# A one-layer language-model tower: the score operands of batch 0 transposed on TensorE instead of restacked by DMA, with unused products between TensorE's work

## The chip, the cores and the metric

One core of a Trainium2 chip runs the program. The metric is the device time of one execution in microseconds (us).

## The reference

For 8 batches of 256 token ids the program looks up rows of 256 in an embedding table, adds a 16-head attention (head width 16, rotary positions) of the normalised rows, and adds a mixture of 8 experts of which the best one by a gate is used.

```python
h = _L0_tok_ref(x, embeddings)                       # rows of the table: (8, 256, 256)
h = h + _L0_attn_ref(_layernorm(h), w_qkv, w_proj)   # q, k rotated; softmax(q k / 4) v; w_proj
h = h + _L0_ffn_ref(_layernorm(h), gate_w, expert_w) # x + expert_w[argmax(gate)] x, x normalised
```

## The kernel before

**The work of one batch.** Each batch has two tiles of 128 tokens (t = 0, 1). GpSimd gathers the rows (`gather`, L321 to L329). VectorE takes the statistics (`f_norm_a`) and, after GpSimd's reciprocal root (`f_rs_of`), scales (`f_norm_b`). TensorE transposes the rows (`x_transpose`, L426). Products are made exact enough by parts: ScalarE rounds to fp32r (`x_high`), VectorE takes the rest (`x_low`), and `product` (L417) adds high by high, low by high and high by low, for two halves of the contraction: six matmuls of 512 columns for `project_qk` of a tile, twelve of 256 columns for `project_v` of a batch.

**Rotation and restack.** `rotate(b, t)` is two VectorE products with the cosine and sine tables out of PSUM (L846, L850), and `rotated_sum` on GpSimd (L342) adds them into `qk`. `qk_transpose` turns it on TensorE (four transposes), `qk_high` and `qk_high_again` on ScalarE and `qk_low` on VectorE fill `parts`, and `restack(b)` (L271), six DMAs of 256 KB from the SP queue, spreads `parts` into `stacks[b % 3]`, where each head of 16 has its high and low parts and a repeat on 48 partitions. In this form one matmul over 48 partitions gives the whole score of a head. Two more rows hold the maxima (`maximum` on SP, or ScalarE's queue for the first) and ones (`ones_rows`).

**Steps, slots and visits.** The steady work is a loop of steps of 16 slots, from step -1. In step b, eight visits (`visit`, L522, one every second slot) each do two heads: the transposed scores of batch b, whose exponentials ScalarE takes (L731), and the plain scores of batch b + 1 into two PSUM banks, whose row maxima VectorE takes (`maximum`, L863). Each bank is written again only when its maximum is out. `max_split`, `max_transpose` and `max_row` turn the negated maxima into rows. Every fourth slot sixteen products of 32 columns make the outputs (`outputs`, L543). Tables (`FRONT`, `EARLY`, `ONE`, `TWO`, L169 to L173) say in which slot each piece of a later batch is issued; each engine runs its own list in order, and waits are on semaphores. Experts of batch b - 2 run in step b, from step 2 on.

**The opening.** Ahead of the loop each engine has a list written out by hand: TensorE L672 to L688, ScalarE L792 ff., VectorE L1002 ff., GpSimd L395 to L408, SP L248 ff. Batches 0, 1 and 2 are projected there. The restack of batch 0 is awaited by the first scores, in step -1:

```python
def scores_wait(b, v, half):
    if v == 0:
        wait(pe, stack_in, b * 96 + 96)
    wait(pe, max_ok, b * NH + 2 * v - half)
```

Step -1 is the scores and maxima of batch 0 alone, step 0 the first with exponentials. `qk_high(1, t)`, which writes `parts` again, waits for the restack of batch 0 (L708).

## Time and profile before

| | us |
|---|---|
| median of three runs | 322.32 |
| lowest and highest | 320.94 and 324.34 |
| the profiled execution | 324.0 |
| its span, first to last instruction | 322.2 |
| TensorE busy in it | 280.8 (87%) |
| VectorE busy | 243.8 (76%) |
| ScalarE busy | 127.0 (39%) |
| GpSimd busy | 85.7 (27%) |

Mean granted clock of TensorE in the profiled execution: 0.944. PE is TensorE's matmuls, PEld its weight loads, DVE VectorE, ACT ScalarE, POOL GpSimd, SP the engine that issues most DMAs; a q behind an engine's name is its instruction queue. L and a number is a line of the kernel. Times count from the first instruction. Busy times are of the engine, and an idle engine costs only where others wait for it.

### The profile page before, as it was taken

To read this page: it belongs to the slowest core of one execution; us is meant where nothing else is said; L and a number is where in the kernel's file an instruction comes from. 1 tells how busy PE (TensorE), PEld (TensorE's weight loads), DVE (VectorE), ACT (ScalarE), POOL (GpSimd) and SP (SyncE) were. 2 spreads that over 40 slices of the span, in tenths; PEclk is the share of its full clock that TensorE was granted. 3 is DMA by queue.
4 is the path that set the end of the run, shared out by engine and by line. 5 is a ranking of instruction groups with operands and counts; after the bars stand their busy time and mean duration, and the time that the engine had idled before them with its cause. 6 is when DMAs were issued, how large, how long until landed. Compare 5 with 4: busy or idle time off the path is not lost.

```text
span 322.2 us, 5465 instructions
## 1 busy us (share of the span) xinstructions
PE 280.8 (87%) x2000; PEld 201.1 (62%) x2000; DVE 243.8 (76%) x595; ACT 127.0 (39%) x261; POOL 85.7 (27%) x96
## 2 busy tenths in 40 slices
PE   0388489888878999989998999999999999999894
PEld 0267367454655777667765776676766766667582
DVE  6766667667798879887997799687988974657663
ACT  3032213643766543345343444353535435330100
POOL 4743500013567402250234113400210210210301
PEclk9999775558999999999999999999999999999998
DMA  4269492480191084015600470039000000001000
GB/s 115 73 247 149 66 161 28 83 119 1 25 161 27 9 142 58 4 36 113 91 6 32 92 117 4 0 94 139 4 33 4 1 28 10 3 1 35 0 33 33
DMA packets 11590, 19.14 MB, mean 59 GB/s; under 512 B 2012, under 2 KB 4903, under 8 KB 11436
## 3 DMA queue, kind: packets, MB, share of 16 engines
q1 hardware_dynamic: 10776, 18.23, 30.4%
q0 software_dynamic: 768, 0.55, 0.7%
q8 instruction: 16, 0.26, 0.3%
q14 instruction: 10, 0.08, 0.1%
q10 hardware_dynamic: 20, 0.02, 0.0%
HBM read 5.30 MB, written 2.10 MB: 23 GB/s over the span
## 4 chain that ended last, share of the span: by engine, by line
PE 47%; DVE 26%; issue 11%; POOL 5%; DMA 4%; ACT 4%; SPq 1%; POOLq 0%; DVEq 0%; ACTq 0%
PE e_bank L422 13%; PE o_bank L552 7%; DVE neg_max L863 7%; PE f_bank L422 7%; DVE acc L942 5%; PE t_pair L517 5%; DMA stacks<-parts 3%; PE s_pair L488 3%; POOL qk L342 2%; PE s_pair L422 2%; PE m_bank L564 2%; PE m_bank L422 2%; POOL res L360 2%; PE o_bank L422 1%; ACT parts L695 1%
## 5 line engine op out<-in xcount | busy, mean ns | idle before, releaser
L731 ACT ACTIVATE probs<-t_pair 128x512 f32<-128x512 f32 x128 | 69.7, 596 | 91.4 <-PE t_pair L517 91.0
L863 DVE TENSOR_REDUCE neg_max<-s_pair 128x2 f32<-128x512 f32 x128 | 82.0, 684 | 15.0 <-PE s_pair L488 15.0
L488 PE MATMUL s_pair<-stacks 48*128 48x256 f32 x256 | 54.8, 341 | 5.8 <-DVE neg_max L863 2.8
L517 PE MATMUL t_pair<-stacks 50*128 50x256 f32 x256 | 50.0, 325 | 2.0 <-DVE neg_max L863 1.7
L517 PEld LDWEIGHTS t_pair<-stacks 50*128 50x128 f32 x256 | 35.5, 199 | 24.4 <-issue 21.4
L422 PE MATMUL e_bank<-ew_h,y_h 128*128 128x512 f32 x92 | 40.3, 439 | 4.6 <-DVE acc L938 2.7
L488 PEld LDWEIGHTS s_pair<-stacks 48*128 48x128 f32 x256 | 38.9, 209 | 8.8 <-DVE neg_max L863 5.0
L552 PE MATMUL o_bank<-probs,vals 128*32 128x256 f32 x512 | 36.4, 405 | 1.2 <-ACT max_rows L695 1.2
L942 DVE SCALAR_TENSOR_TENSOR acc<-e_bank,mask,acc 128x256 f32<-128x256 f32 x66 | 28.9, 479 | 11.2 <-PE e_bank L422 11.2
L422 PE MATMUL e_bank<-ew_h,y_l 128*128 128x512 f32 x92 | 36.3, 395 | 0.0
L422 PE MATMUL e_bank<-ew_l,y_h 128*128 128x512 f32 x92 | 36.3, 395 | 0.0
L342 POOL TENSOR_TENSOR qk<-rope_a,rope_b 128x512 f32<-128x512 f32 x16 | 20.7, 1292 | 49.8 <-DVE rope_b L850 49.7
L422 PEld LDWEIGHTS e_bank<-ew_h,y_h 128*128 128x128 f32 x92 | 17.3, 188 | 12.0 <-DVE acc L942 3.9
L552 PEld LDWEIGHTS o_bank<-probs,vals 128*32 128x32 f32 x512 | 14.0, 113 | 14.9 <-issue 7.5
L422 PE MATMUL f_bank<-wqkv_h,x_h 128*128 128x512 f32 (+1 forms) x44 | 17.2, 390 | 4.7 <-DVE x_l L834 3.8
L349 POOL TENSOR_SCALAR g_ve<-g_mv 128x2 f32<-128x2 f32 x8 | 2.0, 248 | 67.9 <-DVE g_mv L820 67.9
L422 PEld LDWEIGHTS e_bank<-ew_l,y_h 128*128 128x128 f32 x92 | 17.3, 188 | 4.2
L695 ACT ACTIVATE o_t<-o_bank 128x256 f32<-128x256 f32 x32 | 12.4, 389 | 16.1 <-PE o_bank L552 16.1
L335 POOL TENSOR_SCALAR f_ve<-f_mv 128x2 f32<-128x2 f32 x8 | 2.4, 296 | 61.6 <-DVE f_mv L820 61.6
L422 PEld LDWEIGHTS e_bank<-ew_h,y_l 128*128 128x128 f32 x92 | 17.4, 189 | 2.1
L325 POOL DMA_INDIRECT h<-in_emb,ids x16 | 17.2, 1076 | 5.5 <-issue 3.4
L360 POOL TENSOR_TENSOR res<-acc 128x512 f32<-128x512 f32 x8 | 10.2, 1276 | 31.0 <-DVE acc L942 31.0
(132 smaller groups left out, 532.1 us busy)
## 6 DMA issues: line engine op xcount, KB each, us to landing
stacks<-parts SPq DMA_DIRECT2D x48, 256.0 KB, 7.0
ew_raw<-in_expert_w SPq DMA_DIRECT2D x1, 2048.0 KB, 8.2
out<-res SPq DMA_DIRECT2D x8, 256.0 KB, 2.1
probs<-in_w_qkv SPq DMA_DIRECT2D x2, 384.0 KB, 3.8
stacks<-max_rows SPq DMA_DIRECT2D x30, 8.0 KB
h<-in_emb,ids POOLq DMA_INDIRECT x16, 2.6
probs<-in_w_proj SPq DMA_DIRECT2D x1, 256.0 KB, 2.6
stacks<-ones SPq DMA_DIRECT2D x6, 16.0 KB
```

The source lines that it names most:

```text
L325: g.indirect_dma_start(h0[:, j, :], None, emb, bass.IndirectOffsetOnAxis(ap=ids[:, j:j + 1], axis=0), bounds_check=V - 1, oob_is_err=False ...
L342: g.tensor_tensor(qk[:, t, :, :, :].rearrange("p g d j -> p g j d"), rope_a[:, t, :, :].rearrange("p (g j) d -> p g j d", j=8), rope_b[:, ...
L360: g.tensor_tensor(res[:, :, :], acc[:, 0, :, :], acc[:, 1, :, :], ALU.add).then_inc(res_ok, 1)
L422: m = mm(o, a(c), w(c), start=(n == 0), stop=(n == 3 * C - 1))
L488: m = mm(s_pair[:, half, t * N:(t + 1) * N], stacks[b % STACKS][r:r + KS, pair, 0, t * P:(t + 1) * P], stacks[b % STACKS][r:r + KS, pair, ...
L517: m = mm(t_pair[:, half, c * N:(c + 1) * N], stacks[b % STACKS][r:r + KM, pair, 1, c * P:(c + 1) * P], stacks[b % STACKS][r:r + KM, pair, ...
L552: m = mm(o_bank[STRIP * j:STRIP * (j + 1), 0:N], vals[b % VALS][:, c, head(4 * g + j), :], probs[:, (4 * g + j) % RING, c, :], start=(c == ...
L564: m = tr(strips_bank(b, t)[:, g * P:(g + 1) * P], o_t[:, g, t * P:(t + 1) * P], ident[:, :])
L695: return nc.scalar.activation(o, i, ACT.Copy)
L731: nc.scalar.activation(probs[:, (2 * v + half) % RING, :, :].rearrange("p c n -> p (c n)"), t_pair[:, half, :], ACT.Exp, scale=SCALE).then ...
L863: v.tensor_reduce(neg_max[:, k // 4, :, 4 * half + k % 4], s_pair[:, half, :].rearrange("p (t n) -> p t n", t=NT), AX.X, ALU.max, negate=T ...
L942: v.scalar_tensor_tensor(out=acc[:, j, t, :], in0=y, scalar=mask[:, p, t, e:e + 1], in1=base[:, t, :] if u == 0 else acc[:, j, t, :], op0= ...
```

## The change

1. The score operands of batch 0 no longer go through `qk_transpose`, `parts` and `restack(0)`. ScalarE (`z_high`, three copies of 256 elements a tile), VectorE (`z_low`, two subtractions a tile) and GpSimd (`again_k`, one copy a tile) write high, low and repeated parts side by side into `zs` (the memory of `stacks[2]`), with ones beside them. `z_transpose(t)` on TensorE turns 16 blocks a tile into four banks, and eight `z_copy` on ScalarE put them into `stacks[0]`.
2. The restack of batch 1 goes in two halves of four head pairs, six DMAs of 128 KB each, with a semaphore for each; visits 0 and 4 of its scores wait for one each.
3. `fill(o, n)`: n products of 512 columns whose result nobody reads, in TensorE's list: 13 and 4 in the opening, 2 at four further places of it, and 2 behind each visit of step 0.
4. The hand-written lists are reordered: step -1 is now written out between the projections of batches 1 and 2. The rotation, transposes and values of batch 2 move from the opening into slots 0 to 5 of step 0, `proj_weights_low` moves from VectorE to GpSimd, and batch 1's normalised rows use `y_h[0]`, `y_l[0]`.

```diff
+        TWO = dict(rotate0=0, rotate1=1, t0=2, low0=3, t1=3, low1=4, v=5)
...
-            return SLOTS * (k - 2) + table[what] if k and what in table else None
+            table = {2: TWO, 3: EARLY}.get(k, FRONT)
+            return SLOTS * (k - 2) + table[what] if k > 1 and what in table else None
...
+
+        Z_BANKS = [[m_bank, o_bank, f_bank, e_bank], [s_bank[0], s_bank[1], t_bank[1], m_bank]]
+        Z_ORDER = [(0, 0), (0, 1), (1, 0), (1, 1), (1, 2), (0, 2), (0, 3), (1, 3)]
+
+        def z_copied(t, q):
+
+            return Z_ORDER.index((t, q)) + 1
+
+        def z_part(t, k, s):
+
+            return zs[:, :, k, t * P:(t + 1) * P].rearrange("p j (i r) -> p i j r", i=2)[:, :, :, s * HD:(s + 1) * HD]
+
+        def z_from(t, k):
+
+            return qk[:, t, 2 * k:2 * k + 2, :, :].rearrange("p i d j -> p i j d")
...
+            def first_restack():
+
+                sp.wait_ge(qkh_ok, NT)
+                for u in range(2):
+                    for i in range(3):
+                        if i == 1 and u == 0:
+                            sp.wait_ge(again_ok, NT)
+                            sp.wait_ge(qkl_ok, NT)
+                        for half in range(2):
+                            r = 64 * half
+                            sp.dma_start(
+                                stacks[1][r + i:r + KS:3, 4 * u:4 * u + 4, :, :].bitcast(F32).rearrange("d j k n -> d j (k n)"),
+                                parts[64 * u:64 * u + 64, half, 2 * i:2 * i + 2, :].bitcast(F32)).then_inc(half_in[u], 16)
+
...
-                ones_rows(i)
-            restack(0)
+            ones_rows(1)
+            sp.wait_ge(zt_ps, 8)
+            ones_rows(2)
+            first_restack()
...
+                    pool.wait_ge(z_hi, 2 * t + 2)
+                    pool.wait_ge(z_dup_q, t + 1)
+                    pool.wait_ge(z_dup_k, t + 1)
+                    pool.wait_ge(z_lo, 2 * t + 2)
+
...
+            def proj_weights_low():
+                pool.wait_ge(wp_h_ok, 1)
+                g.tensor_tensor(wp_l[:, :, :], wp_raw, wp_h[:, :, :].bitcast(F32), ALU.subtract).then_inc(wp_l_ok, 1)
+
+            def again_k(t):
+                wait(pool, rotated, t + 1)
+                g.tensor_copy(z_part(t, 1, 1), z_from(t, 1)).then_inc(z_dup_k, 1)
 
             def step(b, p):
                 for s in range(SLOTS):
@@ -398,14 +449,15 @@
             gather_tile(3)
             gather(2)
             f_rs_of(1)
+            gate_weights()
+            proj_weights_low()
             rotated_sum(0, 0)
+            again_k(0)
             rotated_sum(0, 1)
+            again_k(1)
             f_rs_of(2)
             rotated_sum(1, 0)
             rotated_sum(1, 1)
-            gate_weights()
-            rotated_sum(2, 0)
-            rotated_sum(2, 1)
             steps(step)
...
+            def fill(o, n):
+
+                for i in range(n):
+                    mm(o[:, :], wqkv_h[:, 0, 0:P], wqkv_h[:, 0, 0:512], start=True, stop=True)
 
+            def z_transpose(t):
+                wait(pe, z_unit, 1)
+                wait(pe, z_lo, 2 * t + 2)
+                wait(pe, z_dup_q, t + 1)
+                wait(pe, z_dup_k, t + 1)
+                if t == 0:
+                    wait(pe, xl_ok, 2)
+                    wait(pe, roped, 2 * NT)
+                for q in range(4):
+                    if t == 1 and q == 2:
+                        wait(pe, roped, 2 * NT + 2)
+                    if t == 1 and q == 3:
+                        wait(pe, z_in, z_copied(0, 0))
+                    for n in range(4):
+                        m = tr(Z_BANKS[t][q][:, n * P:(n + 1) * P].bitcast(F32R),
...
             def scores_wait(b, v, half):
-                if v == 0:
-                    wait(pe, stack_in, b * 96 + 96)
+                if b == 0 and v == 0:
+                    wait(pe, z_in, z_copied(1, 1))
+                elif b == 0 and v in (4, 6):
+                    wait(pe, z_in, max(z_copied(0, v // 2), z_copied(1, v // 2)))
+                elif b == 1 and v % 4 == 0:
+                    wait(pe, half_in[v // 4], 96)
+                elif v == 0:
...
-                    if b == -1 and s == 2:
-                        project_v(2)
+                        if b == 0:
+                            fill(m_bank, 2)
...
             pe.wait_ge(ident_ok, 1)
+            pe.wait_ge(wqkv_h_ok, 1)
+            fill(s_bank[0], 13)
             x_transpose(0)
+            fill(s_bank[0], 4)
             project_qk(0, 0)
+            x_transpose(1)
             project_qk(0, 1)
+            project_qk(1, 0)
+            pe.wait_ge(identr_ok, 1)
+            z_transpose(0)
+            z_transpose(1)
+            visit(-1, 0)
+            project_qk(1, 1)
+            visit(-1, 1)
             project_v(0)
-            x_transpose(1)
-            qk_transpose(0, 0)
-            qk_transpose(0, 1)
-            project_qk(1, 0)
-            project_qk(1, 1)
+            visit(-1, 2)
+            qk_transpose(1, 0)
+            qk_transpose(1, 1)
+            pe.wait_ge(roped, 2 * 2 * NT)
+            fill(t_bank[0], 2)
+            visit(-1, 3)
             project_v(1)
             x_transpose(2)
-            qk_transpose(1, 0)
+            max_transpose(0, 0)
+            visit(-1, 4)
             project_qk(2, 0)
-            qk_transpose(1, 1)
+            visit(-1, 5)
             project_qk(2, 1)
-            pe.wait_ge(identr_ok, 1)
+            visit(-1, 6)
+            fill(t_bank[0], 2)
+            visit(-1, 7)
+            pe.wait_ge(xl_ok, 3)
+            fill(m_bank, 2)
             steps(step)
...
+            def z_high(t):
+                wait(act, rotated, t + 1)
+                for k in range(2):
+                    copy(z_part(t, k, 0), z_from(t, k)).then_inc(z_hi, 1)
+                copy(z_part(t, 0, 2), z_from(t, 0)).then_inc(z_dup_q, 1)
+
+            def z_copy(t, q):
+                wait(act, zt_ps, 4 * t + q + 1)
+                copy(stacks[0][:, 2 * q:2 * q + 2, :, t * P:(t + 1) * P].rearrange("p j k n -> p (j k) n"),
+                     Z_BANKS[t][q][:, :].rearrange("p (m n) -> p m n", m=4)).then_inc(z_in, 1)
...
             x_high(0)
-            values(0)
-            qk_high(0, 0)
-            x_high(1)
-            qk_high(0, 1)
-            qk_high_again(0, 0)
-            qk_high_again(0, 1)
-            values(1)
-            x_high(2)
+            act.wait_ge(gw_in, 16)
+            copy(gw_parts[:, :, 0, :], gw_raw[:, :, :]).then_inc(gw_h_ok, 1)
             act.wait_ge(wp_in, 16)
             copy(wp_h[:, :, :], wp_raw).then_inc(wp_h_ok, 1)
-            act.wait_ge(gw_in, 16)
-            copy(gw_parts[:, :, 0, :], gw_raw[:, :, :]).then_inc(gw_h_ok, 1)
+            x_high(1)
+            z_high(0)
+            z_high(1)
+            for t, q in Z_ORDER:
+                z_copy(t, q)
+            values(0)
+            qk_high(1, 0)
+            qk_high(1, 1)
+            qk_high_again(1, 0)
+            qk_high_again(1, 1)
+            values(1)
+            max_row(0, 0)
+            x_high(2)
             steps(step)
...
+            def z_low(t):
+                for k in range(2):
+                    wait(dve, z_hi, 2 * t + k + 1)
+                    v.tensor_tensor(z_part(t, k, 1 + k), z_from(t, k), z_part(t, k, 0).bitcast(F32),
+                                    ALU.subtract).then_inc(z_lo, 1)
...
+            v.memset(unit[:, :], 1.0).then_inc(filled, 1)
+            dve.wait_ge(filled, 1)
+            v.tensor_copy(zs[:, :, :, :].rearrange("p j k (t i r) -> p (j k t i) r", t=NT, i=2)[:, :, KS:],
+                          unit[:, :].rearrange("p (o r) -> p o r", o=1).broadcast_to([P, 64, HD])).then_inc(z_unit, 1)
+            qkv_weights_low()
             f_norm_a(0)
-            qkv_weights_low()
             f_norm_b(0)
             dve.wait_ge(ident_ok, 1)
             v.tensor_copy(ident_r[:, :], ident[:, :]).then_inc(identr_ok, 1)
+            f_norm_a(1)
+            x_low(0)
+            f_norm_b(1)
             for i in range(VALS):
                 v.memset(vals[i][:, :, :, HD:STRIP], 0.0).then_inc(h_zero, 1)
-            x_low(0)
-            f_norm_a(1)
-            f_norm_b(1)
             rotate(0, 0)
+            x_low(1)
+            f_norm_a(2)
             rotate(0, 1)
-            f_norm_a(2)
-            qk_low(0, 0)
-            x_low(1)
-            qk_low(0, 1)
+            z_low(0)
+            z_low(1)
+            rotate(1, 0)
             f_norm_b(2)
-            rotate(1, 0)
+            maximum(0, 0)
             rotate(1, 1)
+            maximum(0, 1)
+            qk_low(1, 0)
+            maximum(0, 2)
+            qk_low(1, 1)
+            maximum(0, 3)
+            max_split(0, 0)
             x_low(2)
             dve.wait_ge(h_zero, NB + VALS)
             for i in range(VALS):
                 v.memset(vals[i][:, :, :, HD:HD + 1], 1.0).then_inc(filled, 1)
-            proj_weights_low()
-            rotate(2, 0)
-            rotate(2, 1)
+            for k in range(4, VISITS):
+                maximum(0, k)
             steps(step)
```

## Rows read from the trace of the kernel before

**Rows 1.** The page, busy tenths in 40 slices of 8.05 us: TensorE, and its granted clock.
```profile
PE   0388489888878999989998999999999999999894
...
PEclk9999775558999999999999999999999999999998
```

**Rows 2.** Windows of 2 us: length, busy (instructions) by engine, PEclk, DMA share, GB/s.
```profile
34.00:36.00 2.00, 0.00 (x0) 0.00 (x0) 1.29 (x2) 0.00 (x0) 1.45 (x2) 1.00 0.41 65
...
46.00:48.00 2.00, 1.66 (x9) 0.99 (x8) 1.84 (x5) 0.37 (x1) 0.00 (x0) 0.80 1.10 144
...
74.00:76.00 2.00, 2.00 (x25) 1.20 (x18) 1.38 (x3) 0.46 (x1) 0.96 (x1) 0.87 0.00 0
...
78.00:80.00 2.00, 0.60 (x6) 0.36 (x4) 1.97 (x5) 1.44 (x3) 1.26 (x1) 1.00 0.01 4
```

**Rows 3.** The chain that ended last, opening: start us, us, what.
```profile
26.98 9.67 DMA stacks<-parts
```

**Rows 4.** Timeline of the opening: start us, us, engine, line, what [idle before <-releaser].
```profile
11.56 1.57 DVE L1010 MEMSET vals<- 128x512 f32 x3
...
14.11 0.76 PE L422 MATMUL f_bank<-wqkv_h,x_h 128*128 128x512 f32 x1 [1.50 <-DVE x_l L834]
...
16.80 0.63 PE L422 MATMUL e_bank<-wqkv_h,x_h 128*128 128x512 f32 x1
...
21.18 0.75 DVE L817 BATCH_NORM_STATS2 f_st<-h 128x6 f32<-128x256 f32 x2 [0.30 <-DMA h<-in_emb,ids]
...
23.71 18.93 SPq L280 DMA_DIRECT2D stacks<-parts  x12
...
24.09 0.50 PE L422 MATMUL f_bank<-wqkv_h,x_h 128*128 128x512 f32 x1 [1.05 <-DVE x_l L834]
...
25.59 0.40 PE L422 MATMUL e_bank<-wqkv_h,x_h 128*128 128x512 f32 x1
...
25.79 0.69 DVE L846 TENSOR_TENSOR rope_a<-f_bank,rope_sb 128x512 f32<-128x512 f32 x1 [0.52 <-PE f_bank L422]
...
26.40 0.68 DVE L850 TENSOR_TENSOR rope_b<-f_bank,rope_sb 128x512 f32<-128x512 f32 x1
...
28.43 0.60 PE L436 MATMUL m_bank<-ident,xn 128*128 128x128 f32 x4
...
36.79 0.68 PE L488 MATMUL s_pair<-stacks 48*128 48x256 f32 x4 [2.79 <-DMA stacks<-parts]
```

**Rows 5.** Timeline of the end of the opening and step 0.
```profile
47.58 1.91 ACTq L723 DMA_DIRECT2D stacks<-max_rows  x2
...
52.19 0.55 PE L517 MATMUL t_pair<-stacks 50*128 50x256 f32 x1 [0.28 <-DVE neg_max L863]
...
53.52 1.11 PE L477 MATMUL f_bank<-ident,qk 128*128 128x128 f32 x4
...
59.21 1.93 PE L552 MATMUL o_bank<-probs,vals 128*32 128x256 f32 x16
```

**Rows 6.** Timeline, the end of step 0 and the start of step 1.
```profile
77.27 0.38 PE L517 MATMUL t_pair<-stacks 50*128 50x256 f32 x1
...
78.74 1.28 POOL L342 TENSOR_TENSOR qk<-rope_a,rope_b 128x512 f32<-128x512 f32 x1 [2.40 <-DVE rope_b L850]
...
78.78 1.27 DVE L872 TENSOR_TENSOR max_parts<-neg_max,max_parts 128x16 fp32r<-128x16 f32 x1
...
80.73 1.07 PE L552 MATMUL o_bank<-probs,vals 128*32 128x256 f32 x16
```

**Rows 7.** The page's groups: busy us, mean ns | idle before, releaser.
```profile
L863 DVE TENSOR_REDUCE neg_max<-s_pair 128x2 f32<-128x512 f32 x128 | 82.0, 684 | 15.0 <-PE s_pair L488 15.0
...
L342 POOL TENSOR_TENSOR qk<-rope_a,rope_b 128x512 f32<-128x512 f32 x16 | 20.7, 1292 | 49.8 <-DVE rope_b L850 49.7
...
L695 ACT ACTIVATE o_t<-o_bank 128x256 f32<-128x256 f32 x32 | 12.4, 389 | 16.1 <-PE o_bank L552 16.1
```

**Rows 8.** Instructions that touch the stacks: duration ns min/median/max, first and last start.
```profile
L723 ACTq DMA_DIRECT2D stacks<-max_rows x2: 626/938/1251, 47.6 to 48.9; - x2
```

More of the change, by code:

```diff
@@ L147, in tower @@
             sem, "roped rotated qkt_ps qkh_ok qkl_ok again_ok ones_ok".split())
+        z_unit, z_hi, z_dup_q, z_dup_k, z_lo, zt_ps, z_in = map(
+            sem, "z_unit z_hi z_dup_q z_dup_k z_lo zt_ps z_in".split())
         ones_in = sem("ones_in")
+        half_in = [sem("half_in0"), sem("half_in1")]
         stack_in = sem("stack_in")
@@ L196, in steps, with turned_bank, x_parts @@
         def steps(step):
-            for b in range(-1, NB + 2):
+            for b in range(NB + 2):
                 step(b, b % 2)
+        def turned_bank(k, t):
+            return e_bank if early(k) and t == 1 else f_bank
         def front_bank(k, t):
-            return e_bank if early(k) and t == 1 else f_bank
+            return t_bank[t] if k == 1 else turned_bank(k, t)
         def x_bank(k):
             return m_bank if k in (1, 2) else f_bank
-        def turned_bank(k, t):
-            return t_bank[t] if k == 1 else front_bank(k, t)
         def v_bank(k):
-            return o_bank if k < 3 else f_bank
+            return o_bank if k < 2 else f_bank
+        def x_parts(k):
+            return (y_h[0], y_l[0]) if k == 1 else (x_h, x_l)
+        Z_BANKS = [[m_bank, o_bank, f_bank, e_bank], [s_bank[0], s_bank[1], t_bank[1], m_bank]]
[6 more added lines that the diff above has]
+            return qk[:, t, 2 * k:2 * k + 2, :, :].rearrange("p i d j -> p i j d")
         def maxima_slot(b):
@@ L275, in restack @@
                     if i == 1:
[L276 to L277 removed]
+                        wait(sp, again_ok, (b - 1) * NT + NT)
+                        wait(sp, qkl_ok, (b - 1) * NT + NT)
                     for half in range(2):
@@ L302, in ones_rows @@
                     sp.dma_start(stacks[i][r:r + 2, :, 1, :].bitcast(F32), ones[:, :]).then_inc(ones_in, 16)
-            for i in range(STACKS):
-                ones_rows(i)
-            restack(0)
+            ones_rows(1)
+            sp.wait_ge(zt_ps, 8)
+            ones_rows(2)
+            first_restack()
             steps(step)
@@ L439, in project_v @@
             def project_v(b):
-                if b >= 3:
-                    wait(pe, qkl_ok, b * NT + NT)
-                else:
-                    wait(pe, v_ok, b)
+                if b >= 2:
+                    wait(pe, qkl_ok, (b - 1) * NT + NT)
+                elif b == 1:
+                    wait(pe, v_ok, b)
+                else:
+                    pe.wait_ge(z_in, z_copied(0, 1))
+                x_h, x_l = x_parts(b)
                 for t in range(NT):
@@ L472, in qk_transpose @@
                 else:
-                    wait(pe, qkh_ok, b * NT + 1)
-                    wait(pe, qkl_ok, b * NT + 1)
+                    wait(pe, qkh_ok, (b - 1) * NT + 1)
+                    wait(pe, qkl_ok, (b - 1) * NT + 1)
                 wait(pe, rotated, b * NT + t + 1)
@@ L698, in x_high @@
                 wait(act, xt_ps, b + 1)
-                wait(act, v_ps, b)
-                copy(x_h[:, :, :, :].rearrange("p c t n -> p (c t n)"), x_bank(b)[:, :]).then_inc(xh_ok, 1)
+                wait(act, v_ps, 1 if b == 2 else 0 if b == 1 else b)
+                copy(x_parts(b)[0][:, :, :, :].rearrange("p c t n -> p (c t n)"), x_bank(b)[:, :]).then_inc(xh_ok, 1)
             def values(b):
@@ L706, in qk_high @@
             def qk_high(b, t):
-                wait(act, qkt_ps, b * NT + t + 1)
-                wait(act, stack_in, b * 96)
+                wait(act, qkt_ps, (b - 1) * NT + t + 1)
+                if b == 2:
+                    for u in range(2):
+                        wait(act, half_in[u], 96)
+                wait(act, stack_in, (b - 2) * 96)
                 copy(parts[:, :, HIGHS, t * P:(t + 1) * P].rearrange("p i k n -> p k i n"),
@@ L841, in rotate @@
                 wait(dve, qk_ps, b * NT + t + 1)
-                if b == 2:
-                    wait(dve, rotated, 1 * NT + t + 1)
+                if b in (1, 2):
+                    wait(dve, rotated, (b - 1) * NT + t + 1)
                 src = front_bank(b, t)[:, :].rearrange("p (h d) -> p h d", d=HD)
@@ L853, in qk_low @@
             def qk_low(b, t):
-                wait(dve, qkh_ok, b * NT + t + 1)
+                wait(dve, qkh_ok, (b - 1) * NT + t + 1)
                 v.tensor_tensor(parts[:, :, LOWS, t * P:(t + 1) * P].rearrange("p i k n -> p k i n"),
```

63 lines of the change are left out of this document (32 added, 31 removed).

## The prediction

> **What bounds the kernel now.** I read the page's forty slices first, then the chain, the timeline of the opening, and two-microsecond windows.
>
> The slices [rows 1] show TensorE nearly full from about 80 us on, and two weak stretches before it: the opening, in which TensorE is empty or half used, and slices five to nine, in which its granted clock reads 0.7 and 0.5. Behind them nothing is touched by the change, so it can win only ahead of step 1, which begins at 77.27 [rows 6].
>
> The chain [rows 3] says what ends last in the opening: the restack of batch 0, six DMAs of 256 KB, lands 9.67 us after its last issue. The first scores start on it at 36.79 [rows 4]. Step 0 (the first exponentials) starts at 52.19 [rows 5], so the scores of batch 0 alone take 15.4 us and step 0 takes 25.1 us.
>
> The windows [rows 2] show the clock. From 34 to 36 TensorE ran nothing and behind that the clock fell. From 46 to 48, with only score products and two small transposes, it fell again (0.80) although TensorE was busy 1.66 of 2 us. It came back in 74 to 76, behind the projection of batch 3. From 78 to 80 TensorE was busy 0.60 us with transposes, and the clock stayed at 1.00. Of the two levels, 1.2 and 2.4 GHz, step 0 ran nearly whole at the lower one. Ahead of 20 us the record reads 1.00, but six products of 512 columns then took 2.69 us from start to start of the next six (14.11 to 16.80), against 1.50 later (24.09 to 25.59) [rows 4]: that was the lower level too.
>
> **The opening up to the first score.** The restack of batch 0 goes; in its place come rounding on ScalarE and VectorE, 32 transposes, and eight copies. The first fills run where TensorE is empty, so they cost nothing and lift the clock for project_qk(0): that saves 1.2 us for each six products. It isn't on the new path, because VectorE now clears three value tiles (1.57 us [rows 4]) ahead of rotate(0, 0). The new path begins at the gather of batch 2, which landed at about 21.1 (VectorE waited for it) [rows 4], I take it because the load of the expert weights ran beside it, and still does. VectorE's order puts its statistics (0.75, and some 0.2 for the rest) ahead of rotate(0, 1): 22.1. The two rope products take 1.3 [rows 4]: 23.4. GpSimd's sum takes 1.29 [rows 7].
>
> Here z_low(0) on VectorE meets that sum, and both read two SBUF operands. The trace has the case [rows 6]: a VectorE subtraction of 16 elements took 1.27 us because it began 0.04 us behind a GpSimd sum of 1.28. So one of them holds the other; I take z_low's first half (0.4, as the 256-element activation [rows 7]) ahead of the sum and its second half behind it: the sum ends at 25.1, z_low(0) at 25.5. By the Trainium skill (SBUF — State Buffer, Who interferes with whom) such an operation contends with a GpSimd one that reads SBUF and the second is fully blocked; without the rule the sum would be 0.4 us shorter. By it, the trace agrees.
>
> z_high(1) is three activations of 256 elements, 3 x 0.39: 26.3. z_transpose(0) can start at 25.5, with TensorE empty since project_qk(1, 0) ended at about 21.7. No transpose of fp32r between these tiles is in the trace. The nearest rows are four fp32 transposes in 0.60 at the upper level and in 1.11 at the lower one [rows 4, 5]. Bounds for 32: 3 us (nothing but the columns at the rate of the 512-column products) and 8.9 us (32 x 0.28). I take 0.12 each, about a quarter of the 0.60 less the time of the last one's draining, so 3.8 us: 29.3. Six copies overlap them and the fourth is out at 29.1. First scores: 29.4, which is 7.4 us earlier than 36.79.
>
> **From the first score to step 0.** VectorE paces this. Its work from 26.5 is about 16 us: 16 maxima of 0.64 (0.68 alone [rows 7]), two rotations of batch 1 (2.6), two subtractions of 0.7, x_low(2) 0.65, the norm 0.75 and small ones. What it waits for adds 8.6 us. Step by step: the first maximum from 30.0 to 31.2; rotate(1, 1), behind project_qk(1, 1) of 1.5, to 32.9; the next maximum to 34.1; then qk_low(1, 0) stands in line and waits for visit(-1, 2), the transposes (0.6) and ScalarE's copy (0.6), to 35.8. Two subtractions and two maxima: 39.6; the split: 40.0. Now x_low(2) stands in line ahead of the other four maxima. It waits for project_v(1), x_transpose(2) and max_transpose(0, 0) on TensorE (40.7), then on ScalarE for max_row and its two DMA issues (1.91 [rows 5]) ahead of x_high(2): 43.8. x_low ends at 44.4, and project_qk(2, 0) was waiting for it as well. The last four maxima, with two projections between them, take 6.5 us. Step 0 starts at about 50.6: 21.2 us behind the first score instead of 15.4, so 5.8 us of the 7.4 are given back. The restack of batch 1, issued at 36.4 to 44.5, is hidden: the whole restack of batch 0 took 12.9 us from its first issue at 23.71 to its landing at 36.65 [rows 3, 4], so this one is down by 49.4 even from 36.4, and its first half by about 43.5.
>
> **Step 0.** Before, this ran at the lower level. At the upper one three groups of 16 output products save 0.86 each (1.93 and 1.07 [rows 5, 6]), three groups of four transposes 0.5 each, project_qk(3, 0) 1.2, and seven visits, taken to scale like the outputs (1.2 to 0.7), 3.5: in all 8.8 us. Against it stand 16 fills of 512 columns at 0.235 (3.8 us), project_v(2), moved here (12 products of 256 columns, half of the 512-column rate, 1.45), and rotate(2, 0) and (2, 1), also moved here. These hold VectorE 2.6 us and make TensorE wait at visit 1 and, for GpSimd's 1.29, at qk_transpose(2, 1): 2.2 us. 8.8 - 3.8 - 1.45 - 2.2 = 1.3 us saved, 23.8 us. The restack of batch 2 is issued in three steps, the last at about 60.4. The one before needed 12.9 us from the first issue, so it is down by 71, ahead of the end of step 0 at 74.4. gather(3) now runs in step 0, 5 us ahead of its use. proj_weights_low on GpSimd is hidden: GpSimd has nothing between 16 and 19.5.
>
> **Sum.** -7.4 + 5.8 - 1.3 = -2.9 us. The profiled execution took 324.0 (span 322.2), so it would be 321.1; that execution lies 1.7 above the median of 322.32. Beside the median the forecast is 319.4 us.
>
> **Rivals.** 1. The two long waits are shorter than worked out: the gather lands by 20 and ScalarE's DMA issues don't hold x_high(2). For: of the 1.91 the first issue took 1.25 and the second 0.63 [rows 8], so half may be a start-up; against: ScalarE's queue is in order. 1.0 + 1.9 + about 1.1 of the small gaps: -4 us, 315.4.
> 2. Slower: the clock is lost between project_qk(1, 0) and z_transpose(0). TensorE is empty there for some 3.8 us with no fill. For: 34 to 36 [rows 2] was such a gap, and the clock fell. Against: what stands around it here is denser. Then the 32 transposes cost 0.25 each (+4.1), project_qk(1, 1) and project_v(0) 1.2 more each, and visits 0.5: +7.0, 326.4. It decides from 2.9 us on, which the transposes alone exceed.
> The Trainium skill (TensorE: Matmul & The Clock Gate, Part 4: PE-mode transpose) says that transposes don't count as a busy TensorE in the same way. That speaks for this rival. The trace differs in part: from 78 to 80 [rows 2] little but transposes ran and 1.00 was kept. By the rule the time would be 326.4, by the row 319.4.
> 3. The fills don't hold the clock in step 0, so they cost double (7.2 us) and the 8.8 us aren't saved: with the second rival 335 or more.
> 4. The restack in halves moves at half the rate, since each DMA reads 64 partitions. Then its second half lands at about 59, qk_high(2, 0) waits for it, 3 us: 322.4. The kernel before has no such DMA; from 49 to 59 are the bounds.
>
> **How the numbers follow.** Forecast 0.47, rival 1 0.22, rival 2 0.20, rival 3 0.05, rival 4 0.06. The forecast's own range is 317 to 321.5. A measurement here tells about 1%, 3.2 us, from no change: faster means below 319.1. Half of the forecast's cases (0.25) and rival 1 give 0.47; the other half (0.22) and rival 4 give 0.28; rivals 2 and 3 give 0.25. The range 314 to 327 takes in the bounds of the transposes at the upper level and both neighbouring rivals, and leaves out rival 3 and the tails of the first two.
>
> **What would show it.** First score product near 29.4, behind 32 transposes of about 0.12 us; a VectorE wait of over 3 us ahead of x_low(2), released by ScalarE; the first exponentials' products near 50.6; the granted clock at 1.00 through step 0; the second step's first product near 74.4, and from there on the distances of before. A clock of 0.50 at the z transposes shows rival 2; a first score ahead of 28 or no wait at x_low(2) shows rival 1. A step 0 shorter than 22 us would mean that I took too much for the fills and the moved rotations; one over 26 us that the clock was not held.

## The result, and the profile after

| | us |
|---|---|
| after, median of 20 runs | 325.07 (321.53 to 325.98) |
| before, median of 20 runs beside it | 323.97 (319.89 to 325.21) |
| ratio, with its 95% interval | 1.0058 (1.003 to 1.0087) |
| the profiled execution after | 325.86, span 324.1 |
| forecast | 319.4 (314 to 327), faster |

The change costs 0.6%. The forecast was for a gain of 0.9%, so its direction was wrong, though the time lies inside the range. The median of the kernel before is 1.65 us above that of its first three runs, so its profiled execution (324.0) was an ordinary one. The forecast's sum took 1.7 us off for it, without cause as it turns out: beside that execution it came to 321.1, and the profiled execution after took 4.8 us more. In the runs of the kernel before beside the experiments, many times lie near 320.4 us at a mean granted clock of 0.96 or near 324.3 at 0.94, and the median of a set depends on how many of each it has.

Against the starts of [rows 4 to 6], from the two profiled executions:

| start of | before | forecast | after |
|---|---|---|---|
| the first score product | 36.79 | 29.4 | 28.93 |
| step 0 | 52.19 | 50.6 | 55.07 |
| step 1 | 77.27 | 74.4 | 79.50 |

Nearly all of the miss arises between the first score and step 0. That stretch takes 26.1 us, before it was 15.4, and I had worked out 21.2. The two ends of step 0 in the timeline (start us, us, engine, line, what):

```profile
55.07 0.38 PE L605 MATMUL t_pair<-stacks 50*128 50x256 f32 x1
```

```profile
79.50 0.38 PE L605 MATMUL t_pair<-stacks 50*128 50x256 f32 x1
```

Step 0 took 24.4 us between them (25.1 before). The page's slices, as [rows 1]:

```profile
PE   2749859899787999989999999989999999999894
...
PEclk9995878799999999999999999999999999999998
```

TensorE now works from the first slice on. The clock reads 5, 8, 7, 8, 7 in five slices, where it read 7, 7, 5, 5, 5, 8 in six; it still falls. Windows of 2 us, as [rows 2] (length, busy and instructions of PE, PEld, DVE, ACT and POOL, granted clock, DMA share, GB/s):

```profile
22.00:24.00 2.00, 0.00 (x0) 0.00 (x0) 2.00 (x3) 0.00 (x0) 1.38 (x1) 1.00 0.00 0
24.00:26.00 2.00, 1.26 (x10) 1.29 (x11) 1.66 (x3) 1.82 (x4) 1.85 (x4) 0.57 0.00 0
...
30.00:32.00 2.00, 2.00 (x6) 1.48 (x5) 1.05 (x2) 0.60 (x2) 0.00 (x0) 0.50 0.11 29
...
44.00:46.00 2.00, 0.00 (x0) 0.00 (x0) 0.71 (x2) 0.60 (x1) 0.00 (x0) 0.69 0.59 194
46.00:48.00 2.00, 1.96 (x5) 1.58 (x6) 1.27 (x5) 0.00 (x0) 0.00 (x0) 0.50 0.48 154
...
56.00:58.00 2.00, 0.95 (x6) 0.41 (x5) 2.00 (x5) 0.69 (x2) 1.10 (x1) 1.00 0.00 0
58.00:60.00 2.00, 1.90 (x10) 1.34 (x9) 2.00 (x5) 1.20 (x2) 0.89 (x2) 0.60 0.00 0
```

The reader is to see the zero of TensorE in 22 to 24 with a clock that falls behind it (at 24.3), the zero in 44 to 46 with a second fall (at 44.7), and a third fall in 58 to 60 (at 58.4), in step 0, with TensorE busy again after 2 us in which it was busy 0.95. The first two have a price in the chain of what ended last (start us, us, what):

```profile
13.04 7.34 DMA h<-in_emb,ids
...
22.54 2.00 DVE stacks L1071 x2
...
29.73 2.86 PE t_pair L474 x6
...
33.32 2.18 PE o_bank L474 x12
...
42.67 1.23 ACTq L841
...
43.93 0.62 ACTq L841
...
44.66 0.61 ACT x_h L799
...
45.29 0.70 DVE x_l L956
...
46.04 2.93 PE f_bank L474 x6
...
49.70 2.47 PE e_bank L474 x6
```

The gather sits at its head (7.34 us of waiting; before, the gather of batch 2 wasn't on the chain). project_qk(1, 1) takes 2.86 us and project_qk(2, 0) 2.93 us; at the upper level six such products took 1.50 [rows 4]. Between them stand ScalarE's two DMA issues (1.23 and 0.62), then x_high(2) and x_low(2). VectorE's list (start us, us, line, what, [idle before <- releaser]) shows the two places that I had worked out:

```profile
20.40 0.75 DVE L938 BATCH_NORM_STATS2 f_st<-h 128x6 f32<-128x256 f32 x2 [1.14 <-DMA h<-in_emb,ids]
...
22.46 2.07 DVE L1071 TENSOR_TENSOR stacks<-qk,stacks 128x256 fp32r<-128x256 f32 x2
...
45.29 0.69 DVE L956 TENSOR_TENSOR x_l<-m_bank,x_h 128x512 fp32r<-128x512 f32 x1 [4.00 <-ACT x_h L799]
```

The wait ahead of x_low(2) is 4.00 us (worked out 3.8). The two halves of z_low(0), forecast at 0.4 us each, took 2.07 together, because GpSimd's sum stood between them; the two of z_low(1), with no sum between them, took 1.23.

### The profile page after: what moved, and what is told of

Same layout as the page of the kernel before. It is cut to its first block, busy times and chain, and to the rows that moved or that the text cites. A ratio compares the mean times of both kernels' runs of the same rounds, so it can differ in the third digit from the quotient of the medians.

```text
span 324.1 us, 5612 instructions
## 1 busy us (share of the span) xinstructions
PE 286.6 (88%) x2063; PEld 204.8 (63%) x2063; DVE 245.8 (76%) x598; ACT 132.5 (41%) x271; POOL 88.3 (27%) x99
## 4 chain that ended last, share of the span: by engine, by line
PE 47%; DVE 27%; issue 11%; POOL 5%; ACT 4%; DMA 3%; ACTq 1%; POOLq 0%; DVEq 0%
PE e_bank L474 13%; PE f_bank L474 7%; PE o_bank L640 6%; DVE neg_max L985 6%; DVE acc L1064 5%; PE t_pair L605 4%; POOL qk L386 2%; PE s_pair L575 2%; DMA h<-in_emb,ids 2%; PE s_pair L474 2%; PE m_bank L652 2%; PE m_bank L474 2%; POOL res L403 2%; DVE f_st L938 1%; ACT parts L799 1%
## 5 line engine op out<-in xcount | busy, mean ns | idle before, releaser
L575 PE MATMUL s_pair<-stacks 48*128 48x256 f32 x256 | 48.5, 317 | 1.4 <-DVE neg_max L985 1.1
L605 PE MATMUL t_pair<-stacks 50*128 50x256 f32 x256 | 46.5, 308 | 1.6 <-DVE neg_max L985 1.1
L605 PEld LDWEIGHTS t_pair<-stacks 50*128 50x128 f32 x256 | 32.7, 185 | 23.6 <-issue 20.7
L386 POOL TENSOR_TENSOR qk<-rope_a,rope_b 128x512 f32<-128x512 f32 x16 | 21.1, 1316 | 67.6 <-DVE rope_b L972 67.6
L1064 DVE SCALAR_TENSOR_TENSOR acc<-e_bank,mask,acc 128x256 f32<-128x256 f32 x66 | 28.8, 478 | 11.2 <-PE e_bank L474 10.7
L575 PEld LDWEIGHTS s_pair<-stacks 48*128 48x128 f32 x256 | 33.6, 191 | 4.7 <-DVE neg_max L985 2.7
L640 PE MATMUL o_bank<-probs,vals 128*32 128x256 f32 x512 | 34.3, 385 | 1.1 <-ACT max_rows L799 1.1
L474 PE MATMUL f_bank<-wqkv_h,x_h 128*128 128x256 f32 (+1 forms) x46 | 17.0, 370 | 6.6 <-DVE x_l L956 5.5
L799 ACT ACTIVATE o_t<-o_bank 128x256 f32<-128x256 f32 x32 | 12.4, 388 | 16.1 <-PE o_bank L640 16.1
L474 PE MATMUL f_bank<-wqkv_l,x_h 128*128 128x256 f32 (+1 forms) x46 | 15.9, 346 | 0.0
```

Source lines behind the costliest of these rows:

```text
L386: g.tensor_tensor(turned, rope_a[:, t, :, :].rearrange("p (g j) d -> p g j d", j=j), rope_b[:, t, :, :].rearrange("p (g j) d -> p g j d", ...
L474: m = mm(o, a(c), w(c), start=(n == 0), stop=(n == 3 * C - 1))
L575: m = mm(s_pair[:, half, t * N:(t + 1) * N], stacks[b % STACKS][r:r + KS, pair, 0, t * P:(t + 1) * P], stacks[b % STACKS][r:r + KS, pair, ...
L605: m = mm(t_pair[:, half, c * N:(c + 1) * N], stacks[b % STACKS][r:r + KM, pair, 1, c * P:(c + 1) * P], stacks[b % STACKS][r:r + KM, pair, ...
L640: m = mm(o_bank[STRIP * j:STRIP * (j + 1), 0:N], vals[b % VALS][:, c, head(4 * g + j), :], probs[:, (4 * g + j) % RING, c, :], start=(c == ...
L799: return nc.scalar.activation(o, i, ACT.Copy)
```

## The experiments

Ratios are to the kernel before, run beside each set of experiments. Its medians lie between 321.72 and 323.97 us, so ratios are compared, and a median only where it is named as one. A profile shows one execution of each, which can lie 1 to 2 us off its median, and executions of the same instructions can lose the clock at different places (last section), so a profile can differ from another by more than the edit.

**1. Fill the first empty stretch.**

```diff
             project_qk(1, 0)
+            fill(s_bank[0], 14)
             pe.wait_ge(identr_ok, 1)
```

> Edit: 14 unused products of 512 columns between project_qk(1, 0) and z_transpose(0), where TensorE stood empty from 20.98 to 24.74. Clock theory (the 4.5 us that the opening took above the forecast are mostly products at the lower level): the clock stays at 1.00 past 24.26, project_qk(1, 1) takes 1.5 us instead of 2.86 and project_v(0) 1.45 instead of 2.18, so about 2 us less, ratio to the kernel before 1.000. Rival (the waits in VectorE's order set the time, whatever the clock): the time stays at ratio 1.006, since the wait ahead of x_low(2) takes up what is gained.

Measured: 1.0025 (0.9989 to 1.006), against 1.0058. TensorE's timeline in its profile, the fills, the first two groups of four transposes, and the first visits and projection:

```profile
20.98 3.34 PE L481 MATMUL s_pair<-wqkv_h 128*128 128x512 f32 x14
24.66 0.51 PE L558 MATMUL m_bank<-ident_r,stacks 128*128 128x128 f32 x4 [0.34 <-issue]
25.00 0.51 PE L558 MATMUL o_bank<-ident_r,stacks 128*128 128x128 f32 x4
...
28.13 0.51 PE L575 MATMUL s_pair<-stacks 48*128 48x256 f32 x4
28.56 0.51 PE L474 MATMUL t_pair<-wqkv_h,y_h 128*128 128x512 f32 x1
...
30.16 0.51 PE L575 MATMUL s_pair<-stacks 48*128 48x256 f32 x4
```

The clock stayed up and project_qk(1, 1) took 1.60 us from 28.56 to the next visit's start at 30.16, instead of 2.86. The time alone does not decide: the ratios are 0.0033 apart, 1.1 us, which is between the expectation (1.000) and its rival (1.006), and the intervals overlap. VectorE's list says more. In the changed kernel it was done with its work ahead of x_low(2) 12.4 us after the first score (28.93 to 41.29), and here, with the same list, after 10.5 (28.13 to 38.66). The forecast had 10.6.

```profile
42.68 0.69 DVE L957 TENSOR_TENSOR x_l<-m_bank,x_h 128x512 fp32r<-128x512 f32 x1 [4.02 <-ACT x_h L800]
```

**2. Take ScalarE's DMA issues out of the way.** In `max_row`, and in ScalarE's order:

```diff
                 if b == 0 and u == 0:
+                    x_high(2)
                     act.wait_ge(mt_ok, 1)
...
             max_row(0, 0)
-            x_high(2)
             steps(step)
```

> Edit: ScalarE does x_high(2) ahead of the two DMA issues of the first row of maxima, instead of behind them. Theory of the wait: x_high(2) starts at about 42.7 instead of 44.66, x_low(2) and project_qk(2, 0) come 1.9 us earlier; TensorE's empty stretch shrinks from 3.4 to 1.4 us, so that the clock doesn't fall at 44.7 either: 1.9 + 2 = 4 us less, ratio 0.994. If only the wait counts and the clock falls all the same: 1.9 us less, ratio 1.000. Rival (the DMA that lands later than before takes its place, since the row of maxima is needed by visit 0 of step 0): no gain, 1.006.

Measured: 0.9974 (0.9931 to 1.0018), which lies between the first theory's two cases and clear of its rival.

```profile
43.34 0.69 DVE L956 TENSOR_TENSOR x_l<-m_bank,x_h 128x512 fp32r<-128x512 f32 x1 [2.34 <-ACT x_h L799]
```

The wait ahead of x_low(2) is 2.34 us instead of 4.00, so 1.7 of the 1.9 us were saved. In this profile the clock fell all the same, at 40.35, ahead of TensorE's empty stretch in front of project_qk(2, 0), which was down to 0.93 us. The two DMAs do not leave later for it: their issues start at 42.86, beside x_high(2) (42.74) and 0.40 us behind the start of the row's copy, which was 0.41 us before.

**3. Fill the second empty stretch.**

```diff
             visit(-1, 4)
+            fill(t_bank[0], 12)
             project_qk(2, 0)
```

> Edit: 12 unused products of 512 columns between visit(-1, 4) and project_qk(2, 0), where TensorE stood empty from 42.66 to 46.04. Clock theory: no fall at 44.7, project_qk(2, 0) and (2, 1) take 1.5 us instead of 2.8, so 2 to 2.5 us less, ratio 0.999. Rival (VectorE's maxima pace this stretch and hide the products): under 0.5 us, ratio 1.005.

Measured: 1.0018 (0.9973 to 1.0063).

```profile
40.37 3.05 PE L481 MATMUL t_pair<-wqkv_h 128*128 128x512 f32 x12
...
43.03 0.69 DVE L957 TENSOR_TENSOR x_l<-m_bank,x_h 128x512 fp32r<-128x512 f32 x1 [5.03 <-ACT x_h L800]
...
43.77 0.50 PE L474 MATMUL f_bank<-wqkv_h,x_h 128*128 128x512 f32 x1 [0.35 <-DVE x_l L957]
...
45.37 0.50 PE L575 MATMUL s_pair<-stacks 48*128 48x256 f32 x4
45.80 0.50 PE L474 MATMUL e_bank<-wqkv_h,x_h 128*128 128x512 f32 x1
...
47.41 0.50 PE L575 MATMUL s_pair<-stacks 48*128 48x256 f32 x4
...
50.38 0.38 PE L605 MATMUL t_pair<-stacks 50*128 50x256 f32 x1
```

project_qk(2, 0) took 1.60 us (43.77 to 45.37) and (2, 1) 1.6 instead of 2.93 and 2.47. From the start of x_low(2) to step 0 it was 7.35 us (43.03 to 50.38) instead of 9.78 (45.29 to 55.07); the forecast had 6.8. So in the profile the products were on the path, and the maxima did not hide them. The ratio alone lies between the expectation (0.999) and the rival (1.005) and decides nothing. And not all that this profile gained is the edit's. Ahead of the second stretch nothing was changed, yet after the first fall the clock was back at 26.7 here and at 34.5 in the changed kernel, so that the first score came at 27.42 instead of 28.93; and it fell again at 37.0, which made the wait ahead of x_low(2) 5.03 us.

**4. Leave the fills of step 0 out.**

```diff
-                        if b == 0:
-                            fill(m_bank, 2)
```

> Edit: the two unused products behind each visit of step 0 are left out, the others stay. Theory that they hold the clock: without them the clock falls in step 0 and stays down, step 0 takes 26 us or more instead of 24.4, ratio 1.012 or more. Rival (they are a pure cost, 16 x 0.235 us of which some is in front of the next visit): step 0 takes 22 us, ratio 0.999.

Measured: 1.0159 (1.0099 to 1.0219). The windows of its step 0:

```profile
59.00:63.00 4.00, 3.30 (x20) 2.47 (x18) 2.63 (x6) 2.72 (x6) 2.77 (x3) 0.50 0.02 6
63.00:67.00 4.00, 3.74 (x24) 2.99 (x24) 1.84 (x3) 1.94 (x4) 0.66 (x1) 0.50 0.75 151
```

At 0.50 for these 8 us and more, step 0 took 26.8 us (55.55 to 82.38) instead of 24.4. (This profile is of the slowest of the six runs, 330.41; their median is 328.26.) So the fills of step 0 are worth 1% net of their own cost: rival 3 of the prediction fell, and so did the thought that they are a burden.

**5. The three together**: the edits of 1 and 2, and that of 3 with 7 unused products instead of 12.

> Edit: the three together: 14 unused products in the first gap, x_high(2) ahead of ScalarE's two DMA issues, 7 unused products in the second gap. Alone their medians lay 1.55, 3.1 and 2.5 us under the changed kernel's 325.07. Theory (clock and wait are the two causes, and the second gap's clock is bought by either of the last two): 1.5 for the first gap, 1.9 for the wait, 2.2 for the clock of the second gap, together 5.6 us, 319.5 us, ratio 0.987. Rival (one hidden limit, such as VectorE's list, takes up all beyond the first 3 us): 322, ratio 0.996.

Measured: 0.9891 (0.9836 to 0.9947), for 0.987 expected; the median is 319.42, for 319.5. Clear of 1, of the changed kernel and of the rival. The three gains add up (0.0033, 0.0084 and 0.0040 alone, 0.0167 together), so no hidden limit stands behind them. From the first score to step 0 this profile has 21.2 us (27.91 to 49.08), instead of 26.1, with the clock low for 3.4 of them.

**6. Use VectorE's wait as well**, on top of 5.

```diff
             max_split(0, 0)
+            maximum(0, 4)
+            maximum(0, 5)
             x_low(2)
...
-            fill(t_bank[0], 7)
-            project_qk(2, 0)
+            fill(t_bank[0], 2)
             visit(-1, 5)
-            project_qk(2, 1)
+            fill(t_bank[0], 3)
             visit(-1, 6)
-            fill(t_bank[0], 2)
+            project_qk(2, 0)
             visit(-1, 7)
-            pe.wait_ge(xl_ok, 3)
+            project_qk(2, 1)
             fill(m_bank, 2)
```

> Edit: as the three together, and two of VectorE's maxima of batch 0 are put ahead of x_low(2), with visits 5 and 6 ahead of project_qk(2, 0) on TensorE, so that VectorE works in the stretch in which it stood in line. Theory (the step from 28.9 to 55 is set by VectorE's order): step 0 starts 1.2 us earlier than with the three alone, about 318.3 us, ratio 0.983. Rival (project_qk(2, 0), now 1 us later, moves rotate(2, 0) and with it the restack of batch 2): no gain over the three, 0.987.

Measured: 0.9857 (0.98 to 0.9915), for 0.983 expected; the median is 318.25, for 318.3. VectorE's list:

```profile
41.24 2.58 DVE L986 TENSOR_REDUCE neg_max<-s_pair 128x2 f32<-128x512 f32 x4 [2.50 <-PE s_pair L575]
43.73 0.68 DVE L957 TENSOR_TENSOR x_l<-m_bank,x_h 128x512 fp32r<-128x512 f32 x1
```

Four reductions now run where VectorE stood still (the wait ahead of them is 2.50 us, ahead of x_low(2) there is none). The intervals of this and the one before overlap, so the further 1.2 us are likely, not shown.

**7. The halves undone.** `first_restack` issues six whole DMAs, batch 1's rotated sum uses j = 8, and visit 4 waits for nothing.

> Edit: in the changed kernel the restack of batch 1 goes whole again, six DMAs of 256 KB, and visits 0 to 7 of its scores wait for all of them. My theory (it is hidden either way): the restack lands at about 51.5, before step 0 at 55.07, so no change, ratio 1.006. Rival (the halves buy time): the first scores of batch 1 wait for it, step 0 starts at 56 or later, ratio 1.010.

Measured: 1.0067 (1.0021 to 1.0113), as the changed kernel's 1.0058. SP's issues, in the changed kernel and in this one:

```profile
37.67 8.58 SPq L302 DMA_DIRECT2D stacks<-parts  x12
```

```profile
37.83 4.58 SPq L301 DMA_DIRECT2D stacks<-parts  x6
```

Twelve issues take 8.58 us and six take 4.58, but the last transfer of the restack ends near 48 and near 50 us, ahead of step 0 either way, which starts at 55.07 and at 55.16. The halves bring nothing here.

**8. The fills alone, in the kernel before.**

```diff
+            pe.wait_ge(wqkv_h_ok, 1)
+            fill(s_bank[0], 13)
             x_transpose(0)
+            fill(s_bank[0], 4)
...
             pe.wait_ge(identr_ok, 1)
+            fill(s_bank[0], 12)
             steps(step)
...
                         visit(b, s // 2)
+                        if b in (-1, 0):
+                            fill(m_bank, 2)
```

> Edit: the kernel before, with restack(0) and all its order, and only unused products of 512 columns added: 13 and 4 around the first transposes, 12 in the wait for the restack of batch 0, two behind each visit of steps -1 and 0. Clock theory (the kernel before lost about as much to the clock as the transposes win): the clock stays at 1.00 from 37 on, step -1 takes 13 us instead of 15.4 and step 0 20.5 instead of 25.1 with the 3.8 us of fills in it, so 5 to 6 us less, ratio 0.984. Rival (the fills take from the products what the clock gives): ratio 0.998 to 1.002.

Measured: 0.9924 (0.9883 to 0.9966). Some 2.7 us short of what was expected (0.984), yet clear of 1, and better than the whole change.

```profile
34.23 2.93 PE L429 MATMUL s_pair<-wqkv_h 128*128 128x512 f32 x12
37.09 0.51 PE L493 MATMUL s_pair<-stacks 48*128 48x256 f32 x4
...
50.42 0.39 PE L522 MATMUL t_pair<-stacks 50*128 50x256 f32 x1
```

The first score stands where it stood (37.09), the 12 products in front of it carry the clock over the wait, step 0 starts at 50.42, 4.65 us earlier than in the changed kernel, whose first score is 8.16 us earlier. What fell short of the expectation: step 0 took 22.5 (50.42 to 72.95), not 20.5, with one fall of the clock from 57.4 to 60.8 in it, and step -1 13.3, for 13.

**9. No fills at all in the changed kernel**: all six calls of `fill` go.

> Edit: the changed kernel without any of its unused products, so the transposes, halves and new order alone. Theory (fills buy the clock; the order with transposes wins 7.9 us to the first score and gives more back at the lower level): the clock is at the lower level from about 24 to 75, step 0 starts at 57 or later and takes 26.5 us, 331 us, ratio 1.024. Rival (the transposes carry their own weight and the fills are the burden): 322, ratio 0.997.

Measured: 1.0248 (1.0166 to 1.033). Windows of 25 us behind 55, this one and the changed kernel:

```profile
55.00:80.00 25.00, 22.44 (x142) 14.82 (x140) 14.92 (x29) 12.51 (x25) 5.67 (x6) 0.62 0.38 68
```

```profile
55.00:80.00 25.00, 22.86 (x177) 15.22 (x176) 18.48 (x37) 13.36 (x27) 6.95 (x7) 0.93 0.43 68
```

0.62 against 0.93. Transposes, order and halves alone lose 2.5%, and the changed kernel's fills win back 1.9 of it. Its step 0 took 28.6 us (51.50 to 80.14), 2.1 more than expected, while its opening was 5.5 us shorter than I had expected. TensorE's list shows why (the wait ahead of the first transposes, and the first score):

```profile
23.98 0.52 PE L558 MATMUL m_bank<-ident_r,stacks 128*128 128x128 f32 x4 [2.21 <-DVE stacks L1064]
...
27.45 0.50 PE L575 MATMUL s_pair<-stacks 48*128 48x256 f32 x4
```

Without the first fills the projections ran at the lower level up to 19.4 and ended at 21.8, so TensorE stood empty for 2.21 us and not for 3.76, and in this execution the clock read 1.00 from there to 36.6. The first score came 1.5 us earlier than in the changed kernel and step 0 3.6 us earlier. So the loss of this run is not in the opening: it is in step 0 (28.6 us for 24.4) and behind it, where the clock fell once more (0.91 in 80 to 100, 1.00 in the changed kernel).

**10. The gather off the path**, on top of 6, with 7 unused products in the first stretch, which is now shorter.

```diff
             project_qk(1, 0)
-            fill(s_bank[0], 14)
+            fill(s_bank[0], 7)
...
             x_low(1)
-            f_norm_a(2)
             rotate(0, 1)
             z_low(0)
+            f_norm_a(2)
             z_low(1)
```

> Edit: as e6_maxima_in_wait, and VectorE does rotate(0, 1) and z_low(0) ahead of the statistics of batch 2, which wait for a gather until 20.4; 7 instead of 14 unused products in the first gap. Theory (the first score hangs on that gather): first score at 26.2 instead of 28.2 and everything behind it 2 us earlier, 316.3 us, ratio 0.977. Rival (the eight copies and ScalarE's rounding are next in line): 0.5 us at most, 317.8, ratio 0.984.

Measured: 0.9874 (0.9811 to 0.9938), so not different from 6. The expectation of 2 us (0.977) failed.

```profile
20.84 2.51 DVE L1072 TENSOR_TENSOR stacks<-qk,stacks 128x256 fp32r<-128x256 f32 x2 [0.38 <-ACT stacks L800]
23.27 0.74 DVE L939 BATCH_NORM_STATS2 f_st<-h 128x6 f32<-128x256 f32 x2
```

z_low(0) starts 1.6 us earlier than in the changed kernel (20.84 and 22.46) and takes 2.51 us instead of 2.07, then the statistics follow. The first score comes at 27.36, 0.84 earlier than in 6 (28.20). By the chain VectorE worked without a gap from 20.84 to 26.52 (z_low(0) with GpSimd's sum between its halves, the statistics, z_low(1), rotate(1, 0)), and the last eight transposes waited for the end of that. Out of the gather's way, the statistics still stand in VectorE's list ahead of them.

**11. One fill a visit in step 0** (`fill(m_bank, 1)`), on top of 10.

> Edit: as e6_maxima_in_wait, with one unused product behind each visit of step 0 instead of two. Theory (two are needed: with none the changed kernel lost 3.2 us): one isn't enough, the clock falls in step 0 for part of it, 319.5 us, ratio 0.989. Rival (one is enough and each costs up to 0.235 us on the path): 1.5 us less than with two, 316.7, ratio 0.981.

Measured: 0.9871 (0.98 to 0.9942). The run was built on 10 and not on 6, which the expectation names, and is the same as 10 with two fills (0.9874). In its profile the clock fell from 59.8 to 63.2 and came back. Whether one or two are better here stays open.

## Why the prediction was wrong

**The opening up to the first score: right, at 28.93 for 29.4.** The head of the chain was the gather, landed at 20.40 for 21.1. The transposes took 0.51 us for four where I had 0.48, and so 4.2 us in all. z_low's halves took 0.6 us and not 0.4, and z_high(1) 1.83 and not 1.17, but z_high(1) isn't on the chain, and the early gather made up for the rest. But this was at the lower level:

```profile
24.74 0.72 PE L558 MATMUL m_bank<-ident_r,stacks 128*128 128x128 f32 x4 [3.76 <-DVE stacks L1071]
...
28.93 0.80 PE L575 MATMUL s_pair<-stacks 48*128 48x256 f32 x4
```

In experiment 1, at the upper level, four took 0.34 from start to start (24.66 to 25.00). So my 0.12 each was the lower level's price. Rival 2 charged 0.25 each to a lost clock, 4.1 us more; it is 0.04 more each, 1.4 us. That the sum came out is therefore partly luck. Its lower bound for the transposes, 3 us, was wrong as well: at 0.25 us for 512 columns, 32 transposes of 128 columns are 2.0 us, and at the upper level they would take 2.7 (32 x 0.085).

**From the first score to step 0: this step failed.** The forecast had the first score 7.4 us earlier and 5.8 of them given back; it came 7.9 us earlier, and this stretch gave back 10.7 (26.1 instead of 15.4), more than had been won. Its waits were right: the wait at x_low(2) came out within 0.2 us, and x_high(2) behind the DMA issues as worked out. What failed is the term for the projections. Each project_qk was taken at 1.5 us, the upper level (and project_v(0) at none; a project_v is 1.45 in the forecast's step 0), while [rows 2] had shown that an empty stretch is followed by the lower one, and the same step had just worked out two such stretches. By the chain after, project_qk(1, 1) cost 1.36 more, project_v(0) 0.73, project_qk(2, 0) 1.43 and (2, 1) 0.97: 4.5 us, of the 4.9 that this stretch is over the forecast. Experiments 1 and 3 put fills into exactly these stretches and brought the times of the products back, and with 2 they bring the time back (experiment 5). VectorE's lists give nearly the same sum. Up to its wait for x_low(2) the changed kernel was 1.8 us over the forecast, and experiment 1 was on it (12.4, 10.5, forecast 10.6); the wait was 0.2 over; from x_low(2) to step 0 it was 3.0 over, of which 2.4 are gone in experiment 3 (9.78, 7.35, forecast 6.8). Of the 0.55 left, 0.3 is an error of addition: 44.4 and 6.5 are 50.9, not 50.6.

**The second stretch was in no rival.** Rival 2 had the fall, at one place and at 0.20, with 7.0 us. Its place was right: project_qk(1, 1) and project_v(0) cost 2.1 us more there. The other part of its price, 4.1 us for the transposes, is 1.4, and since the forecast had the lower level's price for them without knowing it, that part isn't in the miss. The wait at x_low(2) was in the sum as a wait of VectorE and ScalarE, and nobody asked what TensorE's clock does meanwhile, although [rows 2, 4] showed it falling behind an empty stretch of 2.8 us. That rival 2's 326.4 us lies near the measured time is luck as well: its transposes cost 2.7 us less than it says, and the second stretch, which it lacks, 2.4 us.

**Step 0: nearly right.** 24.4 us for 23.8. One more fall of the clock, at 58.4, is in the 0.6; in the profile of experiment 1, without a fall there, step 0 took 23.8 (51.32 to 75.10). The fills held the clock otherwise, and experiment 4 shows that they must: rival 3 fell. But the terms behind the 23.8 are not all right. With the clock held and the fills in, they make step 0 of the old order 20.1 us (25.1 - 8.8 + 3.8), and experiment 8 had 22.5 there; the changed kernel's moved work then cost 1.9, for 3.65. Two errors of about 2 us offset each other.

**The halves** were hidden, as said; rival 4 fell with the restack down in time, and experiment 7 shows them to be worth nothing.

**Rival 1** fell: the wait at ScalarE's queue was as long as worked out (4.00 for 3.8). The gather did land 0.7 us early, most of the 1.0 that this rival gave it. And its other lever was real. Experiment 2 removed the wait at ScalarE's queue by one moved line.

**What the change is worth in parts.** Without fills it loses 2.5% (experiment 9). The fills bring 1.9% back, and those of step 0 alone 1.0 of it (experiment 4). What the fills of the opening are worth is not shown: experiments 4 and 9 differ by them and their intervals overlap, and in the profiles step 0 starts at 51.50 without them and at 55.07 with them, the clock having held through the first stretch in that profile. Put into the old order they bring 0.8% with none of the new work (experiment 8). The new order with both empty stretches filled and the wait shortened is at 0.9891, and at 0.9857 with the maxima moved (experiments 5 and 6), better than both kernels; experiments 10 and 11 (0.9874, 0.9871) add nothing that can be measured to that. Whether it truly beats the fills alone (0.9924) the overlapping intervals leave open.

## What to carry to other kernels

When a sum of durations passes over a stretch in which TensorE waits, decide for each product behind it at which clock level it runs, and take the duration from a row at that level; every wait that the same sum has found is a candidate. It is no more than that: of the profiles here, some lose the clock in such a stretch and some keep it, so the lower level belongs into the sum as a rival with a price of its own. An operand that arrives earlier wins only as much as the engine that paces the next stretch can use: follow its list, in order, down to the next fixed point before a gain is counted. Unused products are cheap where TensorE would stand still anyway, and they are best tried on the unchanged order first, as the control for everything else.

## What the runs showed of the hardware that was not expected

- A transpose of 128 by 128 in fp32r took 0.085 us each from start to start at the upper level (0.34 for four) and 0.127 at the lower one (0.51 for four). With the end of the last one, four took 0.51 and 0.72 us, and four fp32 transposes 0.60 and 1.11 [rows 4, 5]. So losing the clock costs such transposes much less than it costs fp32 ones or products of 512 columns.
- The clock fell in step 0 of the changed kernel between 58.4 and 61.8 although TensorE was busy 1.90 of 2 us in 58 to 60, with a visit, fills and transposes. It was busy 0.95 in the 2 us before, and its longest empty stretch there was 1.05 us. So a fall can come without a long empty stretch ahead of it, and the 2.21 empty us of experiment 9 brought none.
- Two executions of the same instructions can differ in it. Up to 38 us experiments 1 and 5 have the same work, and TensorE was busy 0.89 of 2 us in 34 to 36 in both. From 36 to 38, below, experiment 1 kept the clock (1.00, the third figure from the end) and experiment 5 did not (0.85):

```profile
36.00:38.00 2.00, 1.90 (x13) 1.56 (x14) 2.00 (x4) 0.05 (x1) 0.00 (x0) 1.00 0.39 131
```

```profile
36.00:38.00 2.00, 1.90 (x12) 1.58 (x11) 2.00 (x4) 0.00 (x0) 0.00 (x0) 0.85 0.40 131
```

- Without the fills of step 0 the clock stood at 0.50 from 59 to 67 (experiment 4).
- A pair of VectorE subtractions that takes 1.23 us undisturbed (z_low(1)) took 2.07 in the changed kernel and 2.51 in experiment 10, because a GpSimd sum got in between its halves, as in [rows 6]. By the Trainium skill (SBUF — State Buffer, Who interferes with whom) one of the two is blocked until the other ends; the traces agree.
